# Attention and expert FFN on one Trainium2 core: score products of neighbouring batches interleaved per head pair

## The chip, the core and the metric

The kernel runs on one core of one Trainium2 chip. The metric is the device time of one execution in microseconds (us), as the median of several runs. The engines are named as in the profile: PE is TensorE (its weight loads are PEld), DVE is VectorE, ACT is ScalarE, POOL is GpSimd, SP is the engine that here only issues DMAs (SPq is its queue, ACTq that of ACT).

## What is computed

Eight batches of 128 x 256 go through a cross attention with 8 heads, whose score scale depends on the batch's token count, and then through a two-expert FFN of which the router picks one expert for each row. In short form (the real code reshapes):

```python
x = x + xcond(layernorm(x), ctx, ctx, itok)      # softmax(s * q.T @ k) per head, s = SCALE * log(itok[b])
logits = layernorm(x) @ w_router.T               # 2 experts
h = einsum('nd,ehd->enh', layernorm(x), w_fc)    # 256 -> 2 x 1024
a = square(where(h >= 0, h, 0.5 * h))
expert_out = einsum('enh,edh->end', a, w_proj)   # 1024 -> 256 for each expert
x = x + (expert_out of the chosen expert) * (its softmax weight)
```

## The kernel before

All products are in float32r, and where precision asks for it an operand is split in two: a rounded part (`_hi`, made by ACT) and a remainder (`_lo`, made by POOL or DVE). An FFN product is thus three matmuls (hi x hi, lo x hi, hi x lo).

**Work of one batch b**, in the names of the code. `load_x(b)` and `load_kv(b)` bring the rows in; `x_moments`, ACT's `x_ln` and `x_rstd`, `x_newton` and `q_normalise(b)` make the normalised, scaled q on DVE; `q_part_hi`, `q_part_lo`, `k_part_hi` and `split_k` split q and k. Six DMAs, `stack_q(b, 0..2)` and `stack_k(b, 0..2)`, put the parts above one another in `q_st` and `k_st` (two buffers each, by b % 2), so that one product over 64 rows gives hi x hi and the cross terms. A stack of batch b waits until `scores_kq(b-2, 3)` has been done. Then, for each of four head pairs g:

- `scores_qk(b, g)` (L1158, four matmuls) writes the scores with queries on the partitions into `snp`, and DVE's `row_max(b, g)` (L723) takes the negated row maximum. In batches 0 and 1 odd pairs use `hp` instead, so two are in flight; from batch 2 on there is one place, and `scores_qk(b, g)` waits for `row_max(b, g-1)`.
- When all four maxima are there, DVE splits them (`split_max_hi`, `split_max_lo`), `max_transpose(b)` (L1168) turns them, ACT's `max_rows(b)` copies them to `mx`.
- `scores_kq(b, g)` (L1182 and L1186, eight matmuls) writes the scores with keys on the partitions into `stp`, the maximum already subtracted, and ACT's `exp(b, g)` (L436) makes `probs`. There is one `stp`: `scores_kq` of the next pair waits for the exp of this one.
- `values(b, e)` (L1202, 16 matmuls) multiplies two pairs' probabilities by v. When both halves are done DVE runs the chain `pv_turn`, `den_inverse`, `attention_out`, `attention_turn`, `x2_sum`, `x2_moments`, (ACT: `y_ln`, `y_rstd`), `x2_newton`, `x2_normalise` (L779), which ends in `x2n`.

**Work of one group g of two batches.** `x_transpose(g)` (L1246) needs x2n of both batches, `xt_part_hi` and `xt_part_lo` split it, then 16 chunks `ffn1(g, c)` (L1218, six matmuls) and 16 chunks `ffn2(g, c)` (L1236, six matmuls). Between them ACT has `leaky` and `square_hi`, POOL `square`, DVE `square_lo`; `expert_out` adds the result with the router's coefficient to `y`. The weights come in eight pieces each (`load_weights`), are rounded by ACT (`split_w`) and their remainder is made by POOL for the first matrix (`split_w`) and DVE for the second (`split_w_lo`).

**What sets the order.** Each engine executes its calls in the order in which they stand in a list written out in the code, one list for SP, POOL, ACT, DVE and PE each; nothing is reordered. An engine whose next call waits for a semaphore lets everything behind it wait too. The wait in `scores_qk` that matters most below is this one (`sets` is 2 in batches 0 and 1, else 1):

```python
wait(pe, s_max, PAIRS * b + (g - sets + 1))
```

and in `scores_kq`, `values` and the stacks:

```python
wait(pe, s_exp, PAIRS * b + g)
pe.wait_ge(s_exp, PAIRS * b + PAIRS // 2 * (e + 1))
wait(q, s_st, PAIRS * (b - 1))
```

## Time and profile before

| | us |
|---|---|
| median of 3 runs | 193.11 (193.11 to 193.41) |
| the profiled execution | 194.08 |
| its span, first to last instruction | 192.3 |
| PE busy | 159.3 |
| DVE busy | 141.2 |
| ACT busy | 97.6 |
| POOL busy | 57.2 |

The profile is of one execution. Its span leaves 1.8 us of that execution's time outside. A line number such as L723 is one of the kernel before. A mean granted TensorE clock of 0.973 stands for the whole span.

### The profile page before, as it was taken

The numbers are of one execution on the slowest core, as the hardware profiler recorded it, in microseconds if no ns is written. First come the engines' busy times: TensorE is split into PE (matmuls) and PEld (weight loads), VectorE is DVE, ScalarE is ACT, GpSimd is POOL, SyncE is SP. The second block draws the span as 40 slices with busy tenths as digits, with TensorE's granted clock in tenths as the row PEclk, the third lists the DMA queues.
The fourth block names the chain that finished last, engine by engine and source line by source line (L and its number), as shares of the span: only waits on it lengthen the run. The fifth ranks groups of instructions, "written<-read, shape, count | busy, mean of one in ns | idle before, by whom it ended". The sixth has DMA issues, their size and how long they took to land.

```text
span 192.3 us, 3953 instructions
## 1 busy us (share of the span) xinstructions
PE 159.3 (83%) x1440; PEld 135.2 (70%) x1440; DVE 141.2 (73%) x313; ACT 97.6 (51%) x179; POOL 57.2 (30%) x66
## 2 busy tenths in 40 slices
PE   0044797533899997999999989999999999999991
PEld 0033554312787685787899869997986999999991
DVE  5688954998789999999999999984278774141421
ACT  3402657943478574297437336562647344344520
POOL 6302354731040622210532402420223223244420
PEclk9999999995599999999999999999999999999999
DMA  4466999973000240421300420000010000010001
GB/s 123 168 221 193 261 309 338 263 248 108 0 31 27 78 143 27 159 65 53 114 2 29 143 78 5 27 2 3 0 55 3 0 0 3 0 55 3 0 0 55
DMA packets 18498, 16.31 MB, mean 85 GB/s; under 512 B 1840, under 2 KB 18352, under 8 KB 18480
## 3 DMA queue, kind: packets, MB, share of 16 engines
q1 hardware_dynamic: 17616, 15.28, 25.5%
q10 hardware_dynamic: 864, 0.79, 1.3%
q8 instruction: 11, 0.18, 0.4%
q14 instruction: 7, 0.06, 0.1%
HBM read 8.72 MB, written 1.05 MB: 51 GB/s over the span
## 4 chain that ended last, share of the span: by engine, by line
PE 51%; DVE 26%; issue 7%; SPq 5%; ACT 5%; DMA 4%; DVEq 0%; ACTq 0%
PE ops L1236 19%; PE hp L1218 18%; DVE negm L723 7%; PE pv L1202 5%; PE stp L1182 4%; DVE a_lo L821 3%; PE snp L1158 3%; DVE wproj_lo L843 2%; DMA cst<-consts 2%; DMA wfc_raw<-w_fc_t 2%; PE stp L1186 2%; ACT probs L436 2%; SPq L137 1%; SPq L168 1%; DVE pvt L742 1%
## 5 line engine op out<-in xcount | busy, mean ns | idle before, releaser
L322 POOL TENSOR_TENSOR a_buf<-l_buf 128x512 f32<-128x512 f32 x32 | 34.7, 1085 | 88.4 <-ACT l_buf L444 65.0
L821 DVE TENSOR_TENSOR a_lo<-a_buf,a_hi 128x512 fp32r<-128x512 f32 x32 | 23.1, 726 | 22.5 <-POOL a_buf L322 22.2
L436 ACT ACTIVATE probs<-stp 128x1024 f32<-128x1024 f32 x32 | 32.8, 1024 | 13.2 <-PE stp L1186 12.3
L1218 PE MATMUL hp<-xt_hi,wfc_hi 128*128 128x256 f32 x128 | 38.6, 301 | 0.4 <-issue 0.4
L1218 PE MATMUL hp<-xt_lo,wfc_hi 128*128 128x256 f32 x128 | 36.5, 285 | 0.0
L1218 PE MATMUL hp<-xt_hi,wfc_lo 128*128 128x256 f32 x128 | 36.4, 285 | 0.0
L723 DVE TENSOR_REDUCE negm<-snp 128x4 f32<-128x1024 f32 x28 | 34.1, 1219 | 3.1 <-PE snp L1158 3.0
L444 ACT ACTIVATE l_buf<-hp 128x512 f32<-128x512 f32 x32 | 19.1, 597 | 33.4 <-PE hp L1218 33.0
L1158 PE MATMUL snp<-k_st,q_st 64*128 64x256 f32 x112 | 14.9, 349 | 20.3 <-DMA q_st<-q_lo 10.8
L1236 PE MATMUL ops<-wproj_hi,a_hi 128*128 128x256 f32 x128 | 27.3, 294 | 0.0
L1218 PEld LDWEIGHTS hp<-xt_hi,wfc_hi 128*128 128x128 f32 x128 | 24.8, 193 | 3.0 <-issue 1.7
L1158 PEld LDWEIGHTS snp<-k_st,q_st 64*128 64x128 f32 x112 | 9.9, 216 | 24.0 <-DMA q_st<-q_lo 10.8
L1236 PE MATMUL ops<-wproj_hi,a_lo 128*128 128x256 f32 x128 | 25.7, 282 | 0.0
L1236 PE MATMUL ops<-wproj_lo,a_hi 128*128 128x256 f32 x128 | 25.7, 281 | 0.0
L1218 PEld LDWEIGHTS hp<-xt_hi,wfc_lo 128*128 128x128 f32 x128 | 24.8, 194 | 0.0
L1182 PE MATMUL stp<-q_st,k_st 64*128 64x256 f32 x128 | 21.4, 348 | 4.0 <-ACT probs L436 3.9
L1218 PEld LDWEIGHTS hp<-xt_lo,wfc_hi 128*128 128x128 f32 x128 | 24.6, 193 | 0.0
L451 ACT ACTIVATE a_hi<-l_buf 128x512 fp32r<-128x512 f32 x32 | 20.1, 630 | 4.2 <-PE ops L1236 3.5
L1236 PEld LDWEIGHTS ops<-wproj_hi,a_hi 128*128 128x128 f32 x128 | 19.6, 189 | 2.4 <-issue 0.8
L1182 PEld LDWEIGHTS stp<-q_st,k_st 64*128 64x128 f32 x128 | 13.4, 204 | 9.8 <-ACT probs L436 5.2
L1236 PEld LDWEIGHTS ops<-wproj_hi,a_lo 128*128 128x128 f32 x128 | 19.7, 188 | 0.0
L1236 PEld LDWEIGHTS ops<-wproj_lo,a_hi 128*128 128x128 f32 x128 | 19.7, 188 | 0.0
(73 smaller groups left out, 220.9 us busy)
## 6 DMA issues: line engine op xcount, KB each, us to landing
k_st<-k_hi SPq DMA_DIRECT2D x16, 128.0 KB, 2.1
wfc_raw<-w_fc_t SPq DMA_DIRECT2D x8, 256.0 KB, 5.4
wproj_raw<-w_proj_t SPq DMA_DIRECT2D x8, 256.0 KB, 5.2
q_st<-q_hi SPq DMA_DIRECT2D x14, 128.0 KB, 2.3
x_raw<-x SPq DMA_DIRECT2D x8, 128.0 KB, 2.9
k_st<-k_lo SPq DMA_DIRECT2D x8, 128.0 KB, 2.1
q_st<-q_lo SPq DMA_DIRECT2D x8, 128.0 KB, 2.1
v_raw<-ctx_t SPq DMA_DIRECT2D x8, 128.0 KB, 2.5
```

What stands on the lines that cost most here:

```text
L322: pool.tensor_tensor(a_buf[d % 2][:, :, :], l_buf[d % 2][:, :, :], l_buf[d % 2][:, :, :], ALU.mult).then_inc(s_a, 1)
L436: act.activation(probs[g][:, :, :, :], stp[:, :, :].rearrange("p e (c n) -> p e c n", c=KC), ACT.Exp).then_inc(s_exp, 1)
L444: act.activation(l_buf[d % 2][:, :, :], hp[:, d % 2, :].rearrange("p (c n) -> p c n", c=2), ACT.Prelu, alpha=0.5).then_inc(s_l, 1)
L451: act.activation(a_hi[d % NA][:, :, :], l_buf[d % 2][:, :, :], ACT.Square).then_inc(s_ahi, 1)
L723: dve.tensor_reduce(negm[b % 2][:, :, :, g].rearrange("p c e -> p e c"), pair[:, :, :].rearrange("p e (c n) -> p e c n", c=KC), AX.X, ALU. ...
L821: dve.tensor_tensor(a_lo[d % NA][:, :, :], a_buf[d % 2][:, :, :], a_hi[d % NA][:, :, :].bitcast(f32), ALU.subtract).then_inc(s_alo, 1)
L843: dve.tensor_tensor(w_piece(w_lo, w, n), w_piece(w_raw, w, n), w_piece(w_hi, w, n).bitcast(f32), ALU.subtract).then_inc(s_wlo[w], 1)
L1158: last = pe.matmul(pair[:, e, qc * KEYS:(qc + 1) * KEYS], q_st[j][rows, g, qc * P:(qc + 1) * P], k_st[j][rows, g, :], start=(qc == 0), sto ...
L1182: pe.matmul(stp[:, e, kc * DIM:(kc + 1) * DIM], k_st[j][rows, g, kc * P:(kc + 1) * P], q_st[j][rows, g, :], start=(kc == 0), stop=False, s ...
L1202: last = pe.matmul(pv[32 * g:32 * g + 32, e * DIM:(e + 1) * DIM], v_one[j][:, kc * HEADS + h, :], probs[h // 2][:, h % 2, kc, :], start=(e ...
L1218: last = pe.matmul(hp[:, d % 2, half], wfc[w][:, kc, c * P:(c + 1) * P], xt[:, kc, :], start=(c % 2 == 0 and kc == 0 and w == 0 and xt is ...
L1236: last = pe.matmul(ops_[:, t * DIM:(t + 1) * DIM], a[d % NA][:, c % 2, t * P:(t + 1) * P], wproj[w][:, c, :], start=(c % CH == 0 and part ...
```

## The change

Nothing is added to or taken from what is computed, and the number of matmuls, vector operations and transfers stays. One wait is new, in `q_normalise`, which now may not overwrite `q_f` of two batches ago before `q_part_lo` has read it:

```diff
             def q_normalise(b):
                 j = b % 2
                 dve.wait_ge(s_xsc, b + 1)
+                wait(dve, s_qlo, b - 1)
                 dve.tensor_scalar(q_f[j][:, :], x_raw[j][:, :], xmv[j][:, 0:1], xsc[j][:, 0:1],
                                   ALU.subtract, ALU.mult).then_inc(s_qf, 1)
```

(From there on a line of the changed kernel has a number one higher.) Everything else is the order of the five lists. On PE `scores_qk(2, g)` stands between `scores_kq(1, g)` instead of behind all of batch 1, `scores_qk(3, g)` between `scores_kq(2, g)`, and so on with each next batch:

```diff
             scores_kq(1, 1)
+            scores_qk(2, 0)
             scores_kq(1, 2)
             values(1, 0)
+            scores_qk(2, 1)
             scores_kq(1, 3)
+            scores_qk(2, 2)
             values(1, 1)
-            scores_qk(2, 0)
-            scores_qk(2, 1)
+            scores_qk(2, 3)
+            max_transpose(2)
+            scores_kq(2, 0)
+            scores_kq(2, 1)
+            scores_qk(3, 0)
             x_transpose(0)
```

`x_transpose(0)` has 30 blocks of PE ahead of it where it had 24; `x_transpose(1)` has 79 in both kernels (one ffn2 more, one scores_qk less among them), `max_transpose(6)` 122 where it had 114, `scores_qk(7, 3)` and `values(7, 1)` about the same. Further places that matter: `values(0, 1)` now stands ahead of `scores_kq(1, 0)`, `scores_qk(1, 0)` behind `scores_kq(0, 0)`.

On ACT the head of the list is:

```diff
             load_len()
+            load_router()
             load_kv(act, 0)
             load_kv(act, 1)
-            load_router()
...
             k_part_hi(0)
-            pick_rows()
-            k_part_hi(1)
             q_part_hi(0)
             stack_q(act, 0, 0)
-            stack_q(act, 0, 1)
+            k_part_hi(1)
             x_ln(1)
             x_rstd(1)
+            stack_q(act, 0, 1)
             q_part_hi(1)
+            pick_rows()
```

and between `exp(1, 1)` and `exp(1, 2)` there are now `k_part_hi(4)` and `q_part_hi(4)`; between `exp(2, 0)` and `exp(2, 1)` there are `y_ln(1)` and `y_rstd(1)`, which before stood far ahead of batch 2's exps. POOL's list splits the weights in the same order with the small steps set otherwise.

**PE, from scores_kq(1, 3) on, before** (stp and mx: scores_kq; snp from k_st and q_st: scores_qk; pv from probs: values; pv from x2n: x_transpose):

```order
L1182 MATMUL stp<-q_st1,k_st1 128x256 x2
L1186 MATMUL stp<-mx1,pick 128x256 x2
L1182 MATMUL stp<-q_st1,k_st1 128x256 x2
L1186 MATMUL stp<-mx1,pick 128x256 x2
L1202 MATMUL pv<-probs2,v_one1 32x256 x2
L1202 MATMUL pv<-probs3,v_one1 32x256 x2
L1202 MATMUL pv<-probs2,v_one1 32x256 x2
L1202 MATMUL pv<-probs3,v_one1 32x256 x2
L1158 MATMUL snp<-k_st0,q_st0 128x256 x8
L1246 MATMUL pv<-cst,x2n0 128x128 x2
L1246 MATMUL pv<-cst,x2n1 128x128 x2
L1158 MATMUL snp<-k_st0,q_st0 128x256 x4
```

and the same place in the changed kernel:

```order
L1159 MATMUL snp<-k_st0,q_st0 128x256 x4
L1183 MATMUL stp<-q_st1,k_st1 128x256 x2
L1187 MATMUL stp<-mx1,pick 128x256 x2
L1183 MATMUL stp<-q_st1,k_st1 128x256 x2
L1187 MATMUL stp<-mx1,pick 128x256 x2
L1159 MATMUL snp<-k_st0,q_st0 128x256 x4
L1203 MATMUL pv<-probs2,v_one1 32x256 x2
L1203 MATMUL pv<-probs3,v_one1 32x256 x2
L1203 MATMUL pv<-probs2,v_one1 32x256 x2
L1203 MATMUL pv<-probs3,v_one1 32x256 x2
L1159 MATMUL snp<-k_st0,q_st0 128x256 x4
L1169 MATMUL snp<-cst,nm_r0 128x128 x2
```

Batch 2's scores (snp) moved in front of, between and behind batch 1's products, and the turn of its maxima follows at once; the transpose of x2n comes after two scores_kq of batch 2.

**DVE, from attention_out(1) to x2_normalise(1), before** (yst, ymv, yvar: x2_moments; yn, ysc: x2_newton; negm: row_max; x2n: x2_normalise; the x names are steps of a later batch's q):

```order
L751 TENSOR_TENSOR att_t<-pvt,den_r 128x2x128
L757 STREAM_TRANSPOSE att<-att_t 128x256
L763 TENSOR_TENSOR x2_1<-x_keep1,att 128x256
L661 BN_STATS yst1<-x2_1 128x6
L664 BN_AGGR ymv1<-yst1 128x2
L667 TENSOR_SCALAR yvar1<-ymv1 128x1
L661 BN_STATS xst0<-x_raw0 128x6
L673 SCALAR_TENSOR_TENSOR yn11<-yrs1,yvar1 128x1
L676 TENSOR_SCALAR yn21<-yn11 128x1
L679 SCALAR_TENSOR_TENSOR ysc1<-yn21,yrs1 128x1
L723 TENSOR_REDUCE negm0<-snp 128x2x2
L779 TENSOR_SCALAR x2n1<-x2_1,ymv1,ysc1 128x256
```

and the first part of the same chain in the changed kernel, from row_max(2, 2) on:

```order
L724 TENSOR_REDUCE negm0<-snp 128x2x2
L743 STREAM_TRANSPOSE pvt<-pv 128x512
L724 TENSOR_REDUCE negm0<-snp 128x2x2
L747 RECIPROCAL den_r<-pvt 128x16
L732 CAST nm_r0<-negm0 128x4x4
L737 TENSOR_TENSOR nm_r0<-negm0,nm_r0 128x4x4
L752 TENSOR_TENSOR att_t<-pvt,den_r 128x2x128
L673 SCALAR_TENSOR_TENSOR yn10<-yrs0,yvar0 128x1
L758 STREAM_TRANSPOSE att<-att_t 128x256
L664 BN_AGGR xmv0<-xst0 128x2
L764 TENSOR_TENSOR x2_1<-x_keep1,att 128x256
L676 TENSOR_SCALAR yn20<-yn10 128x1
```

Batch 1's chain now runs among batch 2's last maxima, the split of these, and the newton steps of batch 0 and of a later x; behind the rows shown come x2_moments(1), x_newton(5), x2_normalise(0), x2_newton(1) and x2_normalise(1).

**SP, the head of the list, before** (cst: consts; k_st and q_st: stacks; the last row is the weights):

```order
L137 DMA x_raw1<-x 128x1x256
L188 DMA cst<-consts 128x132
L160 DMA k_st0<-k_hi0 32x4x256
L160 DMA k_st0<-k_lo0 32x4x256
L160 DMA k_st0<-k_hi0 32x4x256
L168 DMA q_st0<-q_lo0 32x4x256
L160 DMA k_st1<-k_hi1 32x4x256
L160 DMA k_st1<-k_lo1 32x4x256
L160 DMA k_st1<-k_hi1 32x4x256
L176 DMA v_raw0<-ctx_t 128x2x128
```

and in the changed kernel:

```order
L137 DMA x_raw1<-x 128x1x256
L176 DMA v_raw0<-ctx_t 128x2x128
L176 DMA v_raw1<-ctx_t 128x2x128
L188 DMA cst<-consts 128x132
L160 DMA k_st0<-k_hi0 32x4x256
L137 DMA x_raw0<-x 128x1x256
L160 DMA k_st0<-k_lo0 32x4x256
L168 DMA q_st0<-q_lo0 32x4x256
L160 DMA k_st0<-k_hi0 32x4x256
L152 DMA wfc_raw<-w_fc_t 128x2x256 x2
L143 DMA kv_raw0<-ctx_kv 128x1x256
L160 DMA k_st1<-k_hi1 32x4x256
```

Both v loads moved to the front, the last stack_k(0, .) moved behind stack_q(0, 2), and two weight pieces and a context load moved in ahead of batch 1's stacks.

## Rows read from the trace of the kernel before

**Rows 1.** The page, section 1: busy time of each engine.

```profile
PE 159.3 (83%) x1440; PEld 135.2 (70%) x1440; DVE 141.2 (73%) x313; ACT 97.6 (51%) x179; POOL 57.2 (30%) x66
```

**Rows 2.** Stretches: us; busy of PE, PEld, DVE, ACT, POOL; clock; DMA share; GB/s.

```profile
10.84:48.00 37.16, 22.22 (x176) 14.13 (x176) 29.48 (x59) 19.33 (x38) 14.32 (x15) 0.93 0.80 241
...
40.10:46.30 6.20, 0.08 (x4) 0.04 (x2) 5.72 (x16) 2.31 (x7) 1.16 (x2) 0.75 0.53 164
...
48.00:53.10 5.10, 4.44 (x21) 3.64 (x20) 3.45 (x9) 2.54 (x7) 0.00 (x0) 0.50 0.01 2
...
53.10:188.30 135.20, 132.60 (x1246) 117.44 (x1244) 100.81 (x225) 71.64 (x125) 38.43 (x39) 1.00 0.12 39
```

**Rows 3.** Waits (us, times, longest): whole span, then two of PEld from 50 us.

```profile
PEld snp L1158 <- DVE negm L723: 10.4, 6, 6.3
...
PEld snp L1158 <- DVE negm L723: 1.8, 2, 1.2
PEld snp L1168 <- DVE nm_r L736: 1.6, 3, 1.1
```

**Rows 4.** Timeline from 38 to 50 us: start, duration, engine, line, operation.

```profile
38.37 1.29 POOL L315 TENSOR_TENSOR wfc_lo<-wfc_raw,wfc_hi 128x512 fp32r<-128x512 f32 x1
...
38.51 1.30 DVE L779 TENSOR_SCALAR x2n<-x,ymv,ysc 128x256 f32<-128x256 f32 x1
...
38.64 1.07 PE L1202 MATMUL pv<-probs,v_one 128*32 128x256 f32 x16 [1.12 <-ACT probs L436]
...
40.20 0.71 DVE L742 STREAM_TRANSPOSE pvt<-pv 128x512 f32<-128x512 f32 x1
...
46.13 0.40 DVE L779 TENSOR_SCALAR x2n<-x,ymv,ysc 128x256 f32<-128x256 f32 x1
...
46.99 1.11 PE L1246 MATMUL pv<-cst,x2n 128*128 128x128 f32 x4
...
49.56 0.55 PE L1218 MATMUL hp<-xt_hi,wfc_hi 128*128 128x256 f32 x1 [0.38 <-issue]
```

**Rows 5.** Timeline from 7 to 11 us: the last stacks of batch 0, PE's start.

```profile
7.61 1.28 ACTq L168 DMA_DIRECT2D q_st<-q_hi  x2
...
8.38 0.53 SPq L168 DMA_DIRECT2D q_st<-q_lo  x1
...
10.84 0.80 PE L1158 MATMUL snp<-k_st,q_st 64*128 64x256 f32 x4 [10.84 <-DMA q_st<-q_lo]
```

**Rows 6.** Groups of instructions: count, busy us, mean ns, idle before and its releaser.

```profile
L723 DVE TENSOR_REDUCE negm<-snp 128x4 f32<-128x1024 f32 x28 | 34.1, 1219 | 3.1 <-PE snp L1158 3.0
...
L399 ACT ACTIVATE k_hi<-kv_raw 128x256 fp32r<-128x256 f32 x8 | 3.3, 408 | 5.9 <-DMA kv_raw<-ctx_kv 5.8
```

**Rows 7.** Timeline from 19 to 32 us: exp(0,0), values(0,1), exp(1,0).

```profile
19.82 1.02 ACT L436 ACTIVATE probs<-stp 128x1024 f32<-128x1024 f32 x1 [1.61 <-PE stp L1186]
...
31.10 1.93 PE L1202 MATMUL pv<-probs,v_one 128*32 128x256 f32 x16
...
31.20 1.02 ACT L436 ACTIVATE probs<-stp 128x1024 f32<-128x1024 f32 x1 [0.56 <-PE stp L1186]
```

**Rows 8.** Timeline at 56 to 58 us: a score pair between two ffn1 chunks.

```profile
56.26 0.28 PE L1218 MATMUL hp<-xt_lo,wfc_hi 128*128 128x256 f32 x1
...
57.05 0.41 PE L1158 MATMUL snp<-k_st,q_st 64*128 64x256 f32 x4
...
57.38 0.38 PE L1218 MATMUL hp<-xt_hi,wfc_hi 128*128 128x256 f32 x1
```

**Rows 9.** Timeline later: x_transpose(1), max_transpose(6), the last expert_out.

```profile
87.72 0.60 PE L1246 MATMUL pv<-cst,x2n 128*128 128x128 f32 x4
...
112.95 0.44 PE L1168 MATMUL snp<-cst,nm_r 128*128 128x128 f32 x2 [0.86 <-DVE nm_r L736]
...
188.26 0.87 DVE L837 SCALAR_TENSOR_TENSOR y<-ops,coef,y 128x256 f32<-128x256 f32 x2 [1.87 <-PE ops L1236]
```

**Rows 10.** The page, section 6: DMA issues, KB each, median us to landing.

```profile
k_st<-k_hi SPq DMA_DIRECT2D x16, 128.0 KB, 2.1
```

## What is predicted

> **What bounds the kernel now.** I read the page's busy times first, then a table by stretch, then who waited for whom, then the timeline of the first 60 us. TensorE (PE) is busy 159.3 us of 192.3, VectorE (DVE) 141.2; no other engine comes near [rows 1]. The stretches say where PE's missing 33 us lie [rows 2]. Up to 10.84 us PE has nothing [rows 5]. From 10.84 to 48.00 it is busy 22.22 of 37.16 us, and inside that lies a hole, 40.10 to 46.30, with 0.08 us of PE work while DVE is busy 5.72 of 6.20 us. From 48.00 to 53.10 the granted clock is 0.50, which is 1.2 GHz. From 53.10 to 188.30 PE is busy 132.60 of 135.20 us at 1.00, 2.4 GHz. So behind 53 us almost every microsecond is PE work that has to be done somewhere, and only three things can shorten the kernel: an earlier start of the dense part, more of its work already done when it starts, and the few waits left in it.
>
> The hole is a wait for DVE. Scores for the next row maximum have one pair of banks, and its weight loads waited 10.4 us in six places for `row_max`, one of 6.3 us [rows 3]. In the timeline values(1,1) starts at 38.64; DVE then takes the turn of that batch at 40.20, the residual, the norm, and only then `row_max(2,0)`; x2n(1) comes at 46.13, x_transpose(0) at 46.99, ffn1(0,0) at 49.56 [rows 4]. After 50 us weight loads still wait 1.8 us for maxima and 1.6 us for their split; those two are DVE being late [rows 3].
>
> **The first part: the start.** Before, the last stack of batch 0 is issued at 8.38 and PE starts at 10.84, 2.5 us later; the two q_hi stacks leave together at 7.61 [rows 5]. Now `stack_q(0,1)` stands on ACT behind k_part_hi(1), 0.41 us [rows 6], and two steps of one column, x_ln(1) and x_rstd(1), with their issue about 0.9 us, `stack_k(0,2)` stands behind `stack_q(0,2)`, one more issue of 0.5 to 0.6 us, and the first context load stands behind the router's. Whichever lands last, PE starts 0.6 to 1.5 us later; I take 0.9, near the single issue and the ACT work, the nearest rows. The two weight pieces, 512 KB, now go out ahead of batch 1's stacks. I cost them at nothing: those stacks are issued from about 11.7 to 16.5 and wanted only near 20, behind four row maxima of 1.22 us each [rows 6]. If that cover is gone, each us of late landing is a us on the path.
>
> **The second part: the exps of batches 0 and 1.** scores_kq(0,0) no longer stands behind scores_qk(1,0), which gives back 0.6 of the 0.9: exp(0,0) at 20.1 against 19.82 [rows 7]. Then values(0,1) is put ahead of scores_kq(1,0). It needs exp(0,3) and takes 1.93 us at this clock; before, scores_kq(1,0) went first and exp(1,0) ran at 31.20 beside it [rows 7]. I get exp(1,0) at 32.0, 0.8 late. From there each exp is followed by one product of 0.6 us and takes 1.02 us, so exps are 2 us apart as before. One new wait: ACT's q_part_hi(4) needs q_normalise(4), which on DVE is behind pv_turn(0), the residual of batch 0 and two x steps, about 35.5 us; it holds exp(1,2) by some 0.4 us. values(1,1) ends near 40.2, against 39.7 before [rows 4].
>
> **The third part: what fills the hole, and what it costs DVE.** Three scores_qk(2,g) now stand between the products of batch 1, so row_max(2,0) and (2,1) run at 35.5 to 38.7, where DVE had other work or idled. Behind values(1,1) DVE has row_max(2,2), pv_turn(1) from 40.8, row_max(2,3) with its wait for PE, the two splits, and then batch 1's chain with batch 0's newtons and x5's between. The old chain from 40.20 to the end of x2n(1) at 46.53 is 6.3 us [rows 4]; take out row_max(2,0) and the x step (1.6), put in row_max(2,3), splits, x2_newton(0), x2_normalise(0), x_newton(5) and the wait for y_rstd(1), which ACT now has behind exp(2,0): about 3.5 to 4. So 8.2 to 8.7 us, x2n(1) near 49.2, x_transpose(0) at 49.4 against 46.99. Queued behind it on PE are scores_kq(2,2) and scores_qk(3,1), at half clock 1.7 us with the transpose 1.1: **ffn1(0,0) at 52.3 against 49.56, 2.7 us later**.
>
> But ahead of it PE has now done 33 blocks instead of 26: three scores_kq, three scores_qk, one max_transpose more. Such a pair costs the dense part 1.0 us: the last product of a chunk starts at 56.26, of which about 0.11 us is its own slot (256 columns at 2.4 GHz), and the next chunk starts at 57.38 [rows 8]. With the transpose, 3.3 us of work is off the dense part. **Break-even is ffn1(0,0) at 52.9; I expect a lead of 0.6 us there.**
>
> **The fourth part: the dense part.** At x2_normalise(1) DVE's list has three more row maxima (3.5 us), two splits, and steps of x4, x5 and x6: 6.9 us more of its work, at a time 2.7 us later. So DVE is 4 us ahead. That takes away most waits for maxima and splits. Walking both lists to x_transpose(1), which stands behind 79 blocks in both (one qk less, one ffn2 more now), I find few waits up to about 74 us and two new ones, both from DVE's order: scores_qk(5,1) waits near 81.5 for row_max(5,0), which stands behind x2_normalise(2), and x_transpose(1) waits near 84 for x2_normalise(3), behind expert_out(0,0) and row_max(5,0); each about 0.9 us. The transpose starts near 85.7 against 87.72 [rows 9], with 0.35 us more done: 2.3 ahead, 1.7 of it gained here. Later max_transpose(6), which waited 0.86 us, stands eight blocks further back and no longer waits [rows 9]; with ffn products clustered differently I keep 0.4 of it. ACT's and POOL's new orders are costed at nothing: squares and exps hide behind PE's chunks of six such slots, 0.7 us, as long as the lead lasts, and if not they stop ffn2 or a scores_kq. The added wait in `q_normalise` on q_part_lo(b-1) costs nothing where q_lo is done by then, true in list order for every b. The tail after the last product, 188.26 to the end, is the same 4 us [rows 9].
>
> **The sum.** 0.6 + 1.7 + 0.4 = 2.7 us off. The profiled execution took 194.08 us, its span 192.3 and 1.8 around it; it would become 191.4. The median of the runs, 193.11, is 1.0 below that execution, so the forecast is 193.11 - 2.7 = **190.4 us**.
>
> **A rule against the change.** The row: at 38.51 an x2_normalise takes 1.30 us beside POOL's 1.29 us split of weights from 38.37, and both end within 0.2 us; at 46.13 the same form takes 0.40 us with POOL quiet [rows 4]. The Trainium skill, page "SBUF — State Buffer", section "SBUF: two separate sides", says that VectorE and GpSimd hold one port pair exclusively for a whole instruction and that the loser blocks fully. The trace agrees in this pair: the loss is the other's full length, 0.9 us. By the mean durations the sum above stands; by the lock, the new place of the chain beside POOL's splits gives the third rival.
>
> **The rivals.**
> First, **the clock helps as well**. The same sixteen products take 1.93 us at 31.10 and 1.07 at 38.64 [rows 4, 7]: PE rose to 2.4 GHz between them though the granted clock reads 1.00 before too. A denser run of products from 21 us on could raise it some 5 us sooner (about 1.3 us on the path), and scores in the hole could spare the 0.50 of 48.00 to 53.10 (half of 5.1 us, 2.5). All of it gives 186.6, half of it 188.5. Against: PE still has only about 3 us of work between 40 and 49.
> Second, **the moved work is just moved**: x2n(1) comes 0.6 us later than I say and DVE's lead meets new waits worth what it removes: 193.1.
> Third, **slower, by the shared port**: POOL's later weight splits, 1.3 us each, follow ACT's roundings between the exps, and DVE's chain to x2n(1) is now longer. Each meeting costs 0.9 us [rows 4]. I allowed one half of one. Two more put ffn1(0,0) at 54.1, over the break-even of 52.9; three, with the two DVE waits near 81 and 84 grown alike, eat the recovery too: 2.7 - 2.7 - 1.5 gives 194.6. It decides from ffn1(0,0) at about 54.6. For it: one such meeting stood on the old chain, and the new one is 2 us longer. Against: row maxima, the largest part of the added work, read PSUM and mean 1.22 us over all 28 [rows 6].
> Fourth, **it does not interleave**: scores_qk(2,0) needs six stacks that may only start once scores_kq(0,3) is done (about 28), six issues of 0.6 us and 2.1 to land [rows 10], so 34 at the earliest; it stands ahead of scores_kq(1,2). If loads in front hold SP to 31, exps of batch 1 slip 2 to 3 us and the kernel ends near 194.5.
>
> **How the numbers follow.** Forecast case, 189.2 to 191.8: 0.48. Clock: 0.17. Only moved, 192.3 to 193.6: 0.12. Shared port: 0.16. Held stacks: 0.07. Two late starts of 1 to 2 us (first part) widen the upper side. The range 187.0 to 194.6 leaves out a tenth on either side. A measurement here tells 0.2% (0.4 us) from no change. Faster by more: the forecast case, the clock, and the lower edge of the moved case, 0.67. Within: most of the rest of the moved case, 0.08. Slower: its upper edge, the port and the held stacks, 0.25.
>
> **What would show it.** Right: PE's start near 11.7; exp(1,0) near 32; no wait of 6 us for `row_max` any more, the longest under 2.5; x_transpose(0) at 49 to 50 with more blocks in front; waits for maxima and splits behind 50 us below 2 us; x_transpose(1) near 85.7; PE's last product near 185.6. Wrong: ffn1(0,0) after 52.9 without a later recovery, or a start after 12.5, or a stretch behind 60 us in which PE idles for DVE or ACT more than 1 us at a time; or a stretch from 44 to 53 at full clock, which would make the gain larger than said.

## The result, and the profile after

The changed kernel takes **187.44 us**, the median of 4 runs (187.27 to 190.15). The kernel before took 193.26 beside it (193.11 to 194.19, 4 runs). The ratio is 0.9686, 95% interval 0.9645 to 0.9726: 5.8 us less, where 2.7 were forecast. The time lies inside the range, but the gain is twice what was said.

Executions of this kernel take from 185.4 to 190.15 us, so two traces of it are read here. The first is the profiled run of the comparison, which took 190.15 us (span 188.0). The second, called e1_change below, is the same kernel profiled again; it took 185.4 us (span 183.2). The median lies between them.

The page of the changed kernel, section 1 (busy us, share of the span, instructions) and the granted clock in 40 slices, which answers to [rows 1]:

```profile
PE 159.0 (85%) x1440; PEld 136.5 (73%) x1440; DVE 132.0 (70%) x313; ACT 93.4 (50%) x179; POOL 57.7 (31%) x66
...
PEclk9999999755559999999999999999999999999999
```

TensorE does the same work; DVE is busy 9 us less with the same instructions: their own times add up to 3.8 us less, and the rest of the 9 is that more of them overlap in the record. Its stretches, and then those of e1_change (us from the start: length; busy of PE, PEld, DVE, ACT, POOL; clock; DMA share; GB/s), which answer to [rows 2]:

```profile
12.73:48.00 35.27, 24.17 (x186) 15.40 (x188) 26.39 (x61) 17.75 (x37) 12.74 (x13) 0.82 0.60 187
...
51.00:54.15 3.15, 3.15 (x23) 2.37 (x21) 2.54 (x4) 1.93 (x3) 0.00 (x0) 0.50 0.26 65
54.15:85.69 31.54, 31.54 (x310) 26.90 (x309) 28.16 (x68) 20.94 (x41) 8.97 (x11) 0.98 0.31 103
85.69:183.60 97.91, 97.91 (x915) 90.11 (x914) 65.51 (x147) 47.67 (x87) 31.08 (x30) 1.00 0.10 32
```

```profile
12.84:43.00 30.16, 19.02 (x182) 12.60 (x182) 25.17 (x57) 16.96 (x35) 12.76 (x13) 1.00 0.65 209
43.00:50.03 7.03, 5.43 (x37) 4.35 (x36) 5.42 (x19) 4.15 (x8) 0.00 (x0) 0.52 0.59 178
50.03:80.92 30.89, 30.89 (x311) 26.23 (x310) 28.15 (x68) 20.96 (x41) 8.99 (x11) 1.00 0.33 104
```

And the two stretches of the kernel before that stand against the last ones, cut at its own ffn1(0,0) and x_transpose(1):

```profile
49.56:87.72 38.16, 36.61 (x345) 29.97 (x345) 34.56 (x73) 24.54 (x45) 9.65 (x11) 0.95 0.21 67
87.72:188.30 100.58, 99.53 (x918) 90.57 (x916) 68.18 (x158) 48.24 (x84) 28.78 (x28) 1.00 0.08 27
```

A run of the kernel has three parts, bounded by three starts on TensorE: ffn1(0,0), x_transpose(1), and the last product.

| start of | before | forecast | after (188.0) | e1_change (183.2) |
|---|---|---|---|---|
| TensorE | 10.84 | 11.7 | 12.73 | 12.84 |
| x_transpose(0) | 46.99 | 49.4 | 51.53 | 47.41 |
| ffn1(0,0) | 49.56 | 52.3 | 54.15 | 50.03 |
| x_transpose(1) | 87.72 | 85.7 | 85.69 | 80.92 |
| last product | 187.82 | 185.6 (185.1) | 183.53 | 178.80 |
| ffn1(0,0) to x_transpose(1) | 38.16 | 33.4 | 31.54 | 30.89 |
| x_transpose(1) to last product | 100.10 | 99.4 | 97.84 | 97.88 |

The forecast's 185.6 was counted from 188.26, which is the start of DVE's expert_out [rows 9] and not of the last product, 187.82; the same 2.7 us off the last product is the 185.1 in brackets, and the 99.4 goes with it.

So the two traces of the change agree behind ffn1(0,0) within 0.7 us, and differ by 4.1 us ahead of it. There the clock is the difference. The granted clock is 0.50, which is 1.2 GHz, in 35 to 54 us in the one, and only in 43 to 50 in the other: from scores_qk(2,0) to ffn1(0,0) that makes 18.4 us against 15.3. The remaining 1.0 us is there when scores_qk(2,0) starts, at 35.76 and 34.77. It comes mostly from the first products, which run at half pace in both and reach full pace about 2 us later in the first trace: values(0,0), sixteen products, in the first and the second:

```profile
26.00 1.93 PE L1203 MATMUL pv<-probs,v_one 128*32 128x256 f32 x16
...
26.11 1.07 PE L1203 MATMUL pv<-probs,v_one 128*32 128x256 f32 x16
```

The waits of the weight loads behind 54 us, which answer to the last two of [rows 3], in the first trace (us in total, times, longest):

```profile
PEld hp L1219 <- issue: 2.3, 6, 0.4
PEld hp L1219 <- ACT l_buf L444: 0.4, 1, 0.4
PEld snp L1159 <- issue: 0.4, 1, 0.4
PEld stp L1183 <- issue: 0.2, 1, 0.2
```

No wait for DVE is left there, neither the old ones nor the two new ones of the forecast.

### The profile page after: what moved, and what is told of

It is laid out like the page before. It is cut to its first block, busy times and chain, and to the rows that moved or that the text cites. A ratio compares the mean times of both kernels' runs of the same rounds, so it can differ in the third digit from the quotient of the medians.

```text
span 188.0 us, 3959 instructions
## 1 busy us (share of the span) xinstructions
PE 159.0 (85%) x1440; PEld 136.5 (73%) x1440; DVE 132.0 (70%) x313; ACT 93.4 (50%) x179; POOL 57.7 (31%) x66
## 4 chain that ended last, share of the span: by engine, by line
PE 81%; DVE 5%; DMA 5%; ACT 3%; issue 2%; SPq 1%; ACTq 0%; DVEq 0%
PE hp L1219 26%; PE ops L1237 26%; PE pv L1203 10%; PE stp L1183 7%; PE snp L1159 6%; PE stp L1187 4%; DVE negm L724 4%; DMA kv_raw<-ctx_kv 3%; ACT probs L436 2%; PE snp L1169 1%; PE pv L1247 1%; DMA k_st<-k_hi 1%; DMA q_st<-q_lo 1%; SPq L160 1%; PE hp L1159 0%
## 5 line engine op out<-in xcount | busy, mean ns | idle before, releaser
L322 POOL TENSOR_TENSOR a_buf<-l_buf 128x512 f32<-128x512 f32 x32 | 35.9, 1126 | 95.0 <-DVE a_lo L822 53.8
L724 DVE TENSOR_REDUCE negm<-snp 128x4 f32<-128x1024 f32 x28 | 34.2, 1222 | 11.8 <-PE snp L1159 11.7
L1219 PE MATMUL hp<-xt_hi,wfc_hi 128*128 128x256 f32 x128 | 38.2, 298 | 0.0
L1159 PE MATMUL snp<-k_st,q_st 64*128 64x256 f32 x112 | 15.5, 362 | 16.3 <-DMA k_st<-k_hi 12.7
L822 DVE TENSOR_TENSOR a_lo<-a_buf,a_hi 128x512 fp32r<-128x512 f32 x32 | 24.0, 758 | 2.2 <-ACT a_hi L451 2.2
L1159 PEld LDWEIGHTS snp<-k_st,q_st 64*128 64x128 f32 x112 | 10.7, 232 | 20.3 <-DMA q_st<-q_lo 15.1
L1183 PE MATMUL stp<-q_st,k_st 64*128 64x256 f32 x128 | 22.0, 357 | 3.4 <-ACT probs L436 2.5
L451 ACT ACTIVATE a_hi<-l_buf 128x512 fp32r<-128x512 f32 x32 | 19.6, 627 | 6.4 <-PE ops L1237 6.3
L1183 PEld LDWEIGHTS stp<-q_st,k_st 64*128 64x128 f32 x128 | 14.3, 219 | 8.4 <-ACT probs L436 4.4
```

Source lines behind the costliest of these rows:

```text
L322: pool.tensor_tensor(a_buf[d % 2][:, :, :], l_buf[d % 2][:, :, :], l_buf[d % 2][:, :, :], ALU.mult).then_inc(s_a, 1)
L451: act.activation(a_hi[d % NA][:, :, :], l_buf[d % 2][:, :, :], ACT.Square).then_inc(s_ahi, 1)
L724: dve.tensor_reduce(negm[b % 2][:, :, :, g].rearrange("p c e -> p e c"), pair[:, :, :].rearrange("p e (c n) -> p e c n", c=KC), AX.X, ALU. ...
L822: dve.tensor_tensor(a_lo[d % NA][:, :, :], a_buf[d % 2][:, :, :], a_hi[d % NA][:, :, :].bitcast(f32), ALU.subtract).then_inc(s_alo, 1)
L1159: last = pe.matmul(pair[:, e, qc * KEYS:(qc + 1) * KEYS], q_st[j][rows, g, qc * P:(qc + 1) * P], k_st[j][rows, g, :], start=(qc == 0), sto ...
L1183: pe.matmul(stp[:, e, kc * DIM:(kc + 1) * DIM], k_st[j][rows, g, kc * P:(kc + 1) * P], q_st[j][rows, g, :], start=(kc == 0), stop=False, s ...
```

## The experiments

Ratios are against the kernel before, run beside each on the same chip (194.0 to 194.7 us as median), with 95% intervals; the chips differ between experiments. "Middle" is the stretch from ffn1(0,0) to x_transpose(1), "rest" the one from there to the last product.

### Where the gain sits

**e1_change**: the changed kernel, nothing edited.

> The changed kernel as it is, once more, for a second profile and an interval. The profile at hand has the granted clock at 0.50 from 35 to 55 us and a span of 188.0, other executions have 185.1. Theory 'clock' (the early products keep TensorE at 2.4 GHz longer in the usual execution): a profile of a usual execution shows 0.50 only for 5 to 10 us, ffn1(0,0) near 51.5 instead of 54.15, x_transpose(1) near 83 instead of 85.69. Theory 'dense part' (the gain lies in waits that are gone behind 55 us): ffn1(0,0) no earlier than 53, and from x_transpose(1) to the last product 98.3 us as in the profile at hand, against 100.5 before. Time 187.3 to 187.6 by both.

187.29 us, ratio 0.964 [0.9557, 0.9723]; the trace is the one above. Both theories hold in part: 0.50 lasts 7 us and ffn1(0,0) comes at 50.03, even earlier than 'clock' said, and the stretch behind x_transpose(1) is 97.88 us, the same as in the slower trace.

**e2_new_then_old** and **e3_old_then_new** cut both kernels' lists at x_transpose(1): e2 has the new order up to there and the old one behind, e3 the reverse (an entry that the first half has done is left out of the second).

```
# on each of the five engines, A = list of the change, B = list of before
# e2:  A up to x_transpose(1), then what is left of B
# e3:  B up to x_transpose(1), then what is left of A
# e12: A up to ffn1(0, 0), then what is left of B
```

> Changed kernel up to x_transpose(1) on every engine, and behind it what is left in the order of the kernel before. My forecast put 2.3 of 2.7 us before this point and 0.4 behind it. If the order behind it is worth nothing (the lead of VectorE is what removes the waits, whichever list follows): 187.4 to 187.8. If the new order behind x_transpose(1) is itself worth about 2 us (100.5 against 98.3 us in the two profiles): 189 to 190, with waits of TensorE for negm, nm_r or probs back behind 86 us.

> The other half alone: kernel before up to x_transpose(1), behind it what is left in the order of the changed kernel. If the late order is worth nothing: 193.0 to 193.5. If it is worth about 2 us by itself: 191.0 to 191.6.

e2: 191.38 us, 0.9868 [0.9808, 0.9929]; middle 32.5, rest 101.0. e3: 196.36 us, 1.0147 [1.0052, 1.0242], slower than before; middle 39.9, rest 102.0. In e3 the seam itself puts a wait on TensorE (line engine waited for: us, times, longest), and in 92 to 95 us the clock falls behind it:

```profile
PE ops L1237 <- DVE y L831: 2.7, 1, 2.7
```

```profile
92.00:95.00 3.00, 2.21 (x10) 2.24 (x11) 3.00 (x6) 0.00 (x0) 1.04 (x1) 0.60 0.00 0
```

So e2 keeps less than half of the gain and e3 none: a seam of two orders brings waits of its own, as large as the gain that it was to locate.

**e12_new_head** cuts earlier, at ffn1(0,0):

> All engines follow the changed lists up to ffn1(0,0) and the order of before behind it (the work that the changed head has already done left out there). Theory: what the part behind gains up to x_transpose(1) (38.2 to 30.9 us from ffn1(0,0)) comes from the work done early and DVE's lead from it, more than from the new order behind: then x_transpose(1) comes 32 to 34 us behind ffn1(0,0), the time is 188 to 190. Rival: the new order behind 50 us is what removes the waits: 34.5 us or more and 191 to 193, since e2_new_then_old with a later seam (191.4) already lost half of the gain.

192.96 us, 0.9877 [0.9831, 0.9923]; middle 34.8, rest 100.07. The middle is 3.4 us shorter than before even under the old order (38.2 to 34.8). About 1.4 of that is the clock and not the work done early: before, the low clock reaches into this stretch, here it ends with ffn1(0,0), and with the clock at 1.00 the old order takes 36.73 (e8_before_warm, below). The new order behind is worth another 3.9 (to 30.9), of which 1.9 us are a wait for a stack that only this seam makes. Its waits of TensorE's weight loads from 49 to 110 us:

```profile
PEld stp L1183 <- ACT probs L436: 3.1, 7, 1.4
PEld snp L1159 <- DMA q_st<-q_lo: 2.3, 2, 1.7
```

Time and middle fit the rival (34.5 us or more, 191 to 193), though by a wait that belongs to the seam; without its 1.9 us the middle would be 32.9 and fit the theory. That question stays half open. The rest is that of before to 0.03 us: what the rest gained, 2.2 us, belongs to the order behind ffn1(0,0) alone.

### The interleaving, taken out and put in alone

```
# e6_no_interleave, in the change            # e16_interleave_before, in the kernel before
  scores_kq(1, 1)                              scores_kq(1, 1)
- scores_qk(2, 0)                            + scores_qk(2, 0)
  scores_kq(1, 2)                              scores_kq(1, 2)
  values(1, 0)                                 values(1, 0)
- scores_qk(2, 1)                            + scores_qk(2, 1)
  scores_kq(1, 3)                              scores_kq(1, 3)
- scores_qk(2, 2)                            + scores_qk(2, 2)
  values(1, 1)                                 values(1, 1)
+ scores_qk(2, 0) to (2, 2)                  - scores_qk(2, 0) to (2, 2)
```

The row maxima move with them on DVE: in e6 behind pv_turn(1), in e16 ahead of x2_moments(0,0), behind x2_moments(0,2) and ahead of pv_turn(1).

> Changed kernel with the first interleaving undone: scores_qk(2, 0..2) behind values(1,1) on TensorE, row_max(2, 0..2) behind pv_turn(1) on VectorE; all else as in the change. My forecast gave the interleaving 0.6 us at ffn1(0,0), and VectorE's lead of 4 us the rest. If so: x_transpose(0) 2 to 3 us later (3.5 us of maxima are back on VectorE's chain), and the kernel 2 to 3 us slower, 189.5 to 190.5. If the gain comes from the order behind and from the clock: under 1 us slower. If TensorE's hole also brings a longer stretch at 0.50: over 3 us slower.

> The kernel before with the interleaving alone: scores_qk(2,0), (2,1), (2,2) stand ahead of scores_kq(1,2), behind values(1,0) and behind scores_kq(1,3) on TensorE, their row maxima ahead of x2_moments(0,0), behind x2_moments(0,2) and ahead of pv_turn(1) on DVE. Theory: what e6_no_interleave lost (4.9 us) is mostly work put into the idle time ahead of ffn1(0,0); here 24 products of 0.21 us in the slow clock's stretch leave the stretch behind 46 us, while 3.7 us of row maxima stand ahead of x2n(1) on DVE: ffn1(0,0) comes at 50 to 52 us, the time is 1 to 3 us less than before. Rival: the row maxima push x2n(1) and x_transpose(0) back by their whole 3.7 us and the stretch behind gains nothing else: no difference or 1 to 2 us slower, since DVE is busy over 2.5 of 3 us throughout 41 to 50 us.

e6: 192.25 us (10 runs), 0.9929 [0.9878, 0.9981]. Taking the interleaving out loses 4.9 us of the 5.8; ffn1(0,0) comes at 57.31, and middle (30.8) and rest (97.88) stay as in the change. It is the third branch of the expectation that came, with the longer stretch at 0.50:

```profile
33.00:57.30 24.30, 15.17 (x102) 9.50 (x103) 12.95 (x34) 8.96 (x19) 6.04 (x6) 0.51 0.41 120
```

How much of the 4.9 us is this clock and how much the row maxima back on DVE's chain was not separated.

e16: 197.91 us, 1.018 [1.0137, 1.0223], slower. My theory there fell, and the rival named too small a loss. TensorE up to 39 us, and from 40 us on, in e16:

```profile
PE snp L1158 <- DMA q_st<-q_lo: 4.4, 1, 4.4
```

```profile
PE pv L1246 <- DVE x2n L779: 5.5, 1, 5.5
```

scores_qk(2,0) stands ahead of scores_kq(1,2) and waits 4.4 us for a query stack that the old load order brings at 36.7 us; two exps of batch 1 slip, values(1,1) starts at 43.02 instead of 38.64, with it x2n(1) slips, and ffn1(0,0) comes at 52.98. Behind that wait the granted clock is at 0.50 from 36 us on, where it was from 43 us on before. In the change the same wait is 2.2 us, and the scores start at 35.76 (34.77 in e1_change). Start and wait of that product in the change:

```profile
35.76 0.80 PE L1159 MATMUL snp<-k_st,q_st 64*128 64x256 f32 x4 [2.23 <-DMA q_st<-q_lo]
```

So the interleaving pays in the change, where its stacks come earlier, and costs 3.5 us in the kernel before, where they do not. The two differ in DVE's order too, and the interleaving in the kernel before with the new loads was not tried; that the loads decide it is read from the wait.

### The start

```
# e4_old_start: the load order of the kernel before, x(2)'s included, and zero_k(1) ahead of place_v(0) on POOL
# e5_old_start_x2_late: the same, and on DVE and ACT
- x_moments(2, 0) ... x_moments(2, 2), x_ln(2), x_rstd(2) ahead of row_max(0, 0)
+ the same behind split_max_lo(0) and max_rows(0)
```

> Changed kernel with the old start: kv loads ahead of the router's on ACT, stack_q(0,1) right behind stack_q(0,0), batch 0's stacks ahead of both v loads and load_x(2). The profile shows k_hi(0) at 7.32 us (before: 5.10) and TensorE's start at 12.73 (before: 10.84). If this is on the path: start at 10.9 to 11.3 and 185.5 to 186.2 us. If other work absorbs it (row maxima, exps in fixed steps): 187.0 to 187.6.

> As the old start of the changed kernel, and on top x_moments(2, .) on VectorE and x_ln(2), x_rstd(2) on ScalarE moved behind batch 0's maxima. In the old-start run TensorE began at 10.49 but row_max(0,0) only at 14.53, because VectorE waited 2.61 us for x(2) in front of it. If that wait was all that ate the start: row_max(0,0) near 11.5, max_transpose(0) near 16.8 instead of 19.1, and 185.0 to 185.8 us. If what follows sets the pace (stacks of batch 2, exps): max_transpose(0) early, but the first ffn1 where it was, 187 us.

e4: 188.52 us, 0.9745 [0.9673, 0.9817]. e5: 186.92, 0.9666 [0.9542, 0.9791]. TensorE starts 2.2 to 2.5 us earlier, and the time is that of the change or worse. In e4 DVE stands at a load that is now late, ahead of its first row maximum:

```profile
12.45 0.43 DVE L661 BATCH_NORM_STATS2 xst<-x_raw 128x6 f32<-128x256 f32 x1 [2.61 <-DMA x_raw<-x]
```

In e5 that is mended, and the rest is swallowed on the way: scores_qk(2,0) still waits 1.6 us for its stack and starts at 34.90. TensorE's first product is not on the path; the stacks of batch 2 are.

### The clock, taken by itself

```
+ warm(n): n products of 256 columns on constants, into banks that nothing uses yet
# e7_warm: 14 ahead of scores_qk(2, 0), 13 ahead of max_transpose(2), 7 ahead of scores_kq(2, 1)
# e8_before_warm: 46 ahead of scores_qk(2, 1), in the hole of the kernel before
# e9_start_and_warm: e5 and e7 together
```

> Changed kernel with 34 added matmuls of 128x256 into a bank that nothing uses yet, in three gaps of TensorE: 14 ahead of scores_qk(2,0), 13 ahead of max_transpose(2), 7 ahead of scores_kq(2,1). They fit into gaps of 2.0, 1.7 and 1.1 us at 2.4 GHz. Theory 'clock': the granted clock stays at 1.00 behind 30 us, saving half of the 5 to 20 us that the profiles of the change show at 0.50 or near it: 184.5 to 185.8, and less spread between executions. If the clock is not what differs: 187.0 to 187.6, or slower by up to 0.5 where a gap is shorter than what fills it.

> Kernel before with 46 such matmuls, 5.4 us at 2.4 GHz, ahead of scores_qk(2,1), in the hole from 40.1 to 46.3. Theory 'clock': the stretch at 0.50 from 44 to 53.1 is gone, ffn1(0,0) near 49.0, x_transpose(1) 2 to 2.5 us earlier, 190.7 to 191.3 us: of the change's gain of 5.8 us some 2 would then be the clock's. If the clock costs nothing there because waits for VectorE take its place: 193.

> The change with the load order of the kernel before at the start (but x(2) still late, as in e5_old_start_x2_late) and 34 extra 256-column products without use in TensorE's idle gaps before 45 us (as in e7_warm). Theory: the late start and the stretch at 1.2 GHz are two separate losses of the change, neither hidden by the other. Then the time is 183.0 to 184.5, against 184.8 for the change with the extra products alone, the first matmul at 10.4, the granted clock 0.99 or more. Rival: with the clock at 2.4 GHz the wait for the chain exp, values, x2n sets ffn1(0,0), and that chain starts from row_max(0,0), which the early start moves little: then 184.5 to 185.3.

e7: **184.82 us** (183.52 to 185.01), 0.9552 [0.9453, 0.9651]. 34 products that compute nothing make the change 2.5 us faster by the medians, and its runs lie within 1.5 us of one another; all four are below the fastest of the eight runs of the change itself. Three stretches of it against those of e1_change:

```profile
41.00:44.00 3.00, 2.69 (x19) 2.11 (x19) 2.97 (x10) 0.22 (x1) 1.57 (x2) 1.00 0.79 261
44.00:47.00 3.00, 2.68 (x27) 2.20 (x27) 2.50 (x15) 2.14 (x6) 0.00 (x0) 1.00 0.83 242
47.00:50.00 3.00, 2.29 (x21) 1.67 (x20) 2.97 (x5) 2.63 (x4) 0.00 (x0) 1.00 0.39 116
```

```profile
41.00:44.00 3.00, 0.95 (x6) 0.72 (x8) 2.96 (x11) 0.90 (x2) 0.82 (x1) 0.87 0.70 238
44.00:47.00 3.00, 1.88 (x18) 1.58 (x16) 1.98 (x12) 1.32 (x3) 0.00 (x0) 0.50 0.86 260
47.00:50.00 3.00, 3.00 (x22) 2.25 (x18) 2.43 (x4) 1.90 (x3) 0.00 (x0) 0.50 0.36 101
```

Five more traces have the change's order up to ffn1(0,0) (e2, e10, e12, e13, e14). Set beside the others, the time from scores_qk(2,0) to ffn1(0,0) follows the time at 0.50 in front of ffn1(0,0): 14.1 us with none (e7), 15.3 with 6.8 (e1_change), 16.3 to 16.8 with 9.1 to 11.2 (the five), 18.4 with 19.0 (the first trace). In the kernel before it does not: ffn1(0,0) comes at 49.56, 49.54 and 49.45 with 6.4, 11.5 and 11.1 us at 0.50 in front of it (before, e3, e15). For most of that time TensorE waits for DVE there, and the wait takes as long at half clock. The change filled the wait with products, and so made itself sensitive to the clock.

e8: 192.98 us (10 runs), 0.9898 [0.9806, 0.999]; the same treatment gives the kernel before about 2 us by the ratio (0.2 to 3.8 by the interval), less than the 190.7 to 191.3 us expected. Its ffn1(0,0) comes no earlier (49.77), its waits for maxima stay, and what is gained lies behind: the middle, with the clock at 1.00, is 36.73 us instead of 38.16.

```profile
49.77:86.50 36.73, 35.10 (x345) 28.56 (x346) 34.62 (x73) 24.50 (x44) 9.76 (x11) 1.00 0.21 69
```

e9: 185.14 us, 0.9512 [0.9477, 0.9548]: the same as e7 within the intervals. The rival of that expectation held: TensorE starts at 10.43 and exp(0,0) runs at 21.21, where e7 starts at 12.74 and has it at 21.51.

### DVE's lead

The forecast said that DVE is 4 us ahead behind ffn1(0,0) and that this takes the waits away. A delay put on DVE measures the lead: what is swallowed is the lead.

```
+ def busy(n):                      # n memsets of 128x1280, each waiting for the one ahead
+     for i in range(n): ... dve.memset(spare[:, :, :], 0.0).then_inc(s_spare, 1)
# e10_busy_change: busy(3) ahead of row_max(3, 2)     # e14_busy1_change: busy(1)
# e11_busy_before: busy(3) ahead of row_max(3, 0)
# e13_busy_warm: e10 and warm(28) ahead of scores_qk(3, 3)
```

> The change with three memsets of 128x1280 on an unused buffer, waiting for each other (about 1.15 us each, 3.5 us on DVE by the 128x1024 memset's 0.91), just ahead of row_max(3,2) at about 62 us. Theory: behind 50 us DVE works ahead of TensorE in the change (its row maxima wait for score products there), so that the waits of the kernel before are gone; a DVE delay of 3.5 us is then mostly swallowed: x_transpose(1) comes 31 to 32 us behind ffn1(0,0) (30.9 without), and the time grows by 0 to 1 us. Rival: DVE and TensorE go in step and each delay is passed on: 33 to 34.5 us and 2.5 to 3.5 us more.

> The kernel before with the same three memsets ahead of its row_max(3,0), at about 58 us. Theory: DVE is the late one there (TensorE waits for negm 1.8 and nm_r 1.6 us behind 50 us), so the 3.5 us are passed on: x_transpose(1) comes 40.5 to 42 us behind ffn1(0,0) (38.2 without) and the time grows by 2.5 to 3.5 us. Rival: it has as much slack as the change: growth of 0 to 1 us in both, and the waits have another cause than DVE's lateness.

> e10_busy_change (the change with 4.2 us more on DVE ahead of row_max(3,2)) with 28 products without use (256 columns each, about 3.0 us) put ahead of scores_qk(3,3) on TensorE, the place where it waited 3.05 us there. Theory: of the 5.1 us by which e10's stretch from ffn1(0,0) to x_transpose(1) grew (30.9 to 36.0), 3.5 are the wait and 1.6 the stretch at 1.2 GHz that it brought; with TensorE kept busy the wait stays and the clock does not fall, so the stretch is 34.0 to 34.7 us, the granted clock from 59 to 65 us is 1.00, and the time 1 to 2 us under e10's. Rival: the further 1.6 us are work that came late behind the wait (DVE's later steps), and stay: 35.5 us or more.

> e10_busy_change with one memset instead of three: about 1.3 us more on DVE ahead of row_max(3,2). Theory: DVE is only 0.7 us ahead of TensorE there (4.2 us of extra work gave 3.5 us of wait), so TensorE waits about 0.6 us, too short for the clock to fall; the stretch from ffn1(0,0) to x_transpose(1) is 31.3 to 31.8 us and the time 0.4 to 1.0 us over the change's. Rival: more of the delay is swallowed on the way (0 to 0.2 us), or a wait of any length brings the lower clock with it (then 32.3 us or more).

e10: 192.95 us, 0.9937 [0.9884, 0.9989], 5.6 us over the change; middle 36.0 instead of 30.9. e11: 199.54, 1.0243 [1.0204, 1.0282], 4.8 us over before; middle 44.4 instead of 38.2. Both expectations fell, and the theory of the lead with them: the three memsets take 4.2 us with their gaps, and both kernels pass on more than that. The place in e10, and the clock behind it (L1168 there is scores_qk, as the edit moved the lines):

```profile
54.63 1.12 DVE L858 MEMSET spare<- 128x1280 f32 x1 [0.21 <-issue]
56.09 1.12 DVE L858 MEMSET spare<- 128x1280 f32 x1 [0.33 <-DVE spare L858]
57.55 1.12 DVE L858 MEMSET spare<- 128x1280 f32 x1 [0.33 <-DVE spare L858]
```

```profile
59.81 0.80 PE L1168 MATMUL snp<-k_st,q_st 64*128 64x256 f32 x4 [3.05 <-DVE negm L726]
```

```profile
59.00:62.00 3.00, 2.19 (x20) 1.09 (x20) 2.84 (x7) 0.00 (x0) 0.00 (x0) 0.62 0.14 47
62.00:65.00 3.00, 3.00 (x27) 2.60 (x20) 1.59 (x6) 0.92 (x3) 0.58 (x1) 0.81 0.79 210
```

In e13 the wait is filled with products, and the same stretches read:

```profile
59.00:62.00 3.00, 3.00 (x34) 2.15 (x33) 2.16 (x6) 0.00 (x0) 0.00 (x0) 1.00 0.26 87
62.00:65.00 3.00, 3.00 (x32) 2.87 (x31) 2.60 (x10) 1.92 (x6) 1.58 (x2) 1.00 0.82 203
```

The middle as a whole mixes in the clock near 50 us, which differs from run to run (e13's is 35.5, the bound that its rival named). The piece around the delay does not: from scores_qk(3,2) to max_transpose(3) it is 5.19 us in e1_change (52.25 to 57.44), 9.81 in e10, 8.74 in e13, 5.55 in e14, and from max_transpose(3) to x_transpose(1) the four agree within 0.02 us (23.47 to 23.49). It falls into two parts at scores_qk(3,3), the product that waits:

| us | e1_change | e14 | e10 | e13 |
|---|---|---|---|---|
| scores_qk(3,2) to scores_qk(3,3) | 2.22 | 2.60 | 5.36 | 5.78 |
| scores_qk(3,3) to max_transpose(3) | 2.97 | 2.95 | 4.45 | 2.96 |

So of 4.2 us of delay 1.1 is swallowed in e10 and 3.1 is passed on, and the clock adds 1.5 behind it, which e13 does not pay. (e13's first part says nothing of the delay: its 28 products run until 60.30, 1.0 us after row_max(3,2) is done at 59.28.) e13 took 190.93 us, 0.9811 [0.9748, 0.9874], 2.0 under e10. e14: 187.94 us, 0.9647 [0.9592, 0.9702], middle 31.6: of 1.3 us of delay 0.4 is passed on, 0.9 is swallowed, and the clock stays at 1.00 (the rest of its longer middle is the low clock, which ends at 51 us there and at 50 in e1_change). **DVE's lead in the change, at this place, is 0.9 to 1.1 us, not 4.**

Why could it not be 4? Each score product of one head pair waits for the row maximum of the pair before, since they share one pair of banks. However early DVE is, it waits for TensorE at the next one, as it does for 11.7 us in all in the first trace (8.6 in e1_change):

```profile
L724 DVE TENSOR_REDUCE negm<-snp 128x4 f32<-128x1024 f32 x28 | 34.2, 1222 | 11.8 <-PE snp L1159 11.7
```

That is 3.0 us in [rows 6]. A lead along the list of an engine is bounded by the buffers between it and the engine that it leads.

### max_transpose(6) alone

```
# e15_before_mt6, the kernel before, TensorE
- max_transpose(6)
  ffn2(1, 1)
  ffn1(1, 9)
+ max_transpose(6)
```

> The kernel before with max_transpose(6) moved two blocks back on TensorE (behind ffn2(1,1) and ffn1(1,9)), nothing else. Theory: its wait of 0.86 us for nm_r is a wait for a DVE result that comes on its own time, so the move takes it away and nothing is late behind it: from x_transpose(1) to the last product 99.2 us instead of 100.1, the time 0.6 to 0.9 us less (ratio 0.995 to 0.997). Rival: max_rows(6), exp(6,0) and scores_kq(6,1) then come late and the wait returns there: 99.8 to 100.3 us, no difference.

193.25 us (12 runs), 0.9932 [0.9898, 0.9965]; rest 99.07 instead of 100.10. As expected: one entry moved by two blocks gives 1.03 us of trace, the whole wait of [rows 9] and a little more. The product has no wait any more:

```profile
113.59 0.38 PE L1168 MATMUL snp<-cst,nm_r 128*128 128x128 f32 x2
```

## Why the prediction was wrong, step by step

**The start (first part): missed by 1.0 us, and it did not matter.** 12.73 instead of 11.7, past the 12.5 that the text had named as a sign of error. My 0.9 leaned on one more issue and on ACT's work, and gave the context load's new place behind the router's no size of its own; k_hi(0) now waits for that load and runs at 7.32 us, where it ran at 5.10:

```profile
7.32 0.42 ACT L399 ACTIVATE k_hi<-kv_raw 128x256 fp32r<-128x256 f32 x1 [1.95 <-DMA kv_raw<-ctx_kv]
```

e4, e5 and e9 show that the loss is covered.

**The exps (second part): right at its end.** exp(0,0), said at 20.1, runs at 21.4 by the late start and by a split of its maxima that takes 0.53 us at 18.22, beside POOL, where 0.17 is usual; but exp(1,0), said at 32.0, stands at 31.72. That is luck: I let values(0,1) take 1.93 us, as before, and it took 1.07, because TensorE had reached full pace by then.

**The hole (third part): filled as said, but what ends it is another thing.** x_transpose(0) was said at 49.4 and came at 51.53 and 47.41, ffn1(0,0) at 52.3 and came at 54.15 and 50.03: that the forecast lies in the middle of the two traces is luck as well. It let DVE's chain to x2n(1) set the time. In both traces DVE waits in that chain for y_rstd(1) (1.15 and 0.91 us), which stands on ACT behind exp(2,0), and is done 0.2 us ahead of x_transpose(0). TensorE meanwhile goes without a gap from scores_kq(2,1), which waits for the same exp, over scores_qk(3,0) to x_transpose(0):

```profile
49.95 0.58 PE L1183 MATMUL stp<-q_st,k_st 64*128 64x256 f32 x2 [1.11 <-ACT probs L436]
...
50.89 0.41 DVE L780 TENSOR_SCALAR x2n<-x,ymv,ysc 128x256 f32<-128x256 f32 x1
...
50.97 0.63 PE L1159 MATMUL snp<-k_st,q_st 64*128 64x256 f32 x4
51.53 1.11 PE L1247 MATMUL pv<-cst,x2n 128*128 128x128 f32 x4
```

Products and exps lie on this path now, and so the clock does. The text treated the 1.2 GHz of 48.00 to 53.10 as fixed. It moves by run, and with it 3 to 4 us.

**The dense part (fourth part): the step that failed.** It held two terms, 1.7 us up to x_transpose(1) and 0.4 behind. The first had two waits in it that do not come and left out the clock; the second was too small.
- Up to x_transpose(1) the forecast's stretch was 33.4 us; it is 30.9 to 31.5. The forecast took 3.0 us of work out of it (three pairs and a transpose less, 0.35 more for an ffn2) and 1.7 of waits: the 3.4 of [rows 3] less two new ones. Against e8_before_warm, the old order with the clock at 1.00, the 7.3 us that e1_change gains here come apart. The clock is 1.4 (38.16 to 36.73). The work is 2.5: three scores_kq, four scores_qk and a max_transpose less and one ffn2 more, at the 0.58, 0.34, 0.14 and 0.72 us that TensorE goes forward by each in these traces. What is left, 3.3, are waits. So the old waits were sized well and the work 0.5 too high, and two things were wrong. Before, 49.56 to 53.10 ran at 1.2 GHz [rows 2] on work of this stretch, for which the forecast had nothing; in the change the low clock ends at 50 to 56 us, at or shortly behind ffn1(0,0) and mostly on other work. And I added two new waits of 0.9 us each, at scores_qk(5,1) and x_transpose(1): neither came. In e1_change the x2n that x_transpose(1) needs is done at 79.99, 0.9 us ahead of it:

```profile
79.57 0.42 DVE L780 TENSOR_SCALAR x2n<-x,ymv,ysc 128x256 f32<-128x256 f32 x1
```

- The reason given, a DVE lead of 4 us, was false (e10, e14). That the old waits went because the new order puts enough products between a row maximum and the score product that needs it, place by place, is argued and not shown: e12 has other waits back when the new head runs under the old order, but part of them are the seam's.
- Behind x_transpose(1) I kept 0.4 of max_transpose(6)'s 0.86 us. Alone it is worth 1.03 (e15). The rest of the 2.2 us, 1.2, is not taken apart by a run. By the lists 0.4 of it is work, the ffn2 that now stands ahead of x_transpose(1) for a scores_qk behind it, which the forecast had as 0.35. For the other 0.8 the trace of before offers a wait of 0.6 us for probs, 0.1 more for a split maximum and 0.4 of issue (weight loads, us in total, times, longest, from 87.72 us):

```profile
PEld snp L1168 <- DVE nm_r L736: 1.2, 2, 1.1
...
PEld pv L1202 <- ACT probs L436: 0.6, 1, 0.6
PEld snp L1168 <- issue: 0.4, 1, 0.4
```

**The sum.** For the slower of the two traces: ffn1(0,0) 4.6 later instead of 2.7, middle 6.6 shorter instead of 4.8, rest 2.3 shorter instead of 0.7: 4.3 off the last product. x_transpose(1) was met to 0.01 us by two errors that cancel. For the faster trace, 0.5 later, 7.3 and 2.2 shorter: 9.0 off. The measured gain of 5.8 lies between. Behind ffn1(0,0) both traces gain 3.4 to 4.0 us more than was said; ahead of it the one is 1.9 us later than said and the other 2.2 earlier.

**The rivals.** The clock was the one that held in part: the forecast case with half of it gives 188.5, all of it 186.6, and 187.4 was measured. But it does not help as I put it. The change does not spare the low clock. It moves it out of the middle, and ahead of ffn1(0,0), where it cost the kernel before nothing, it now costs up to 4 us by how long it lasts. e7 shows that all of it is worth 2.5 us more. The shared port cost nothing on the chain to x2n(1), where the rival had it: both x2n steps on the chain (48.70 and the 50.89 above) take 0.41 us with POOL quiet, where [rows 4] had 1.30.

```profile
48.70 0.41 DVE L780 TENSOR_SCALAR x2n<-x,ymv,ysc 128x256 f32<-128x256 f32 x1
...
46.00:51.00 5.00, 2.96 (x20) 2.28 (x22) 3.71 (x21) 2.22 (x5) 0.00 (x0) 0.50 0.74 211
```

The rule of the Trainium skill, page "SBUF — State Buffer", section "SBUF: two separate sides", that the two hold the port for a whole instruction, is borne out elsewhere in the change. 18 DVE instructions of the first trace run more than 0.15 us and 30% over the median of their kind, each beside a POOL instruction, 9.6 us in all; before it was 23 and 12.1. The clearest is a step of one column that takes 0.22 us at 50.25 and 1.01 here, and ends within 0.02 us of POOL's:

```profile
80.09 1.04 POOL L322 TENSOR_TENSOR a_buf<-l_buf 128x512 f32<-128x512 f32 x1 [3.54 <-ACT l_buf L444]
80.14 1.01 DVE L673 SCALAR_TENSOR_TENSOR yn<-yrs,yvar 128x1 f32<-128x1 f32 x1
```

Row maxima are not among them (mean 1.22 us in both kernels). None of the 18 made TensorE wait behind ffn1(0,0), where no wait for DVE is left; ahead of it one is the split of batch 0's maxima at 18.22, for which TensorE did wait, 0.4 us longer than without it. The held stacks were real but small: scores_qk(2,0) waits 2.2 us for its stack, against 34 us named as the earliest start; 34.77 and 35.76 were seen. e16 shows what it costs when it is larger.

## What to carry to other kernels

A wait of TensorE can have two prices: its length, and the time at 1.2 GHz behind it. Where the profile shows the granted clock at 0.50 behind a gap, ask what work now stands in that time, and try a few products without use in the gap before reordering anything: they gave 2.5 us here, nearly half of what a whole new order gave. Before a lead of one engine is written into a sum, look for the buffer that bounds it. And count the clock's stretches as something that moves with the work ahead of them: of the two traces of the change one is 4.8 us longer, and the clock is all that was found to differ. A low clock was free here while TensorE waited for DVE, and had its price once the wait was filled with products.

## What the runs showed of the hardware

- **Short and long waits.** Behind a wait of 0.3 us (e14) the granted clock stays at 1.00; behind 3.05 us (e10) it reads 0.62 and 0.81 in 59 to 65 us and costs 1.5 us; behind 4.64 us (e11) 0.92, 0.50, 0.50 and 0.94 in 59 to 71 us, and the middle grows by 6.2 us for 4.2 of delay. The Trainium skill, page "TensorE: Matmul & The Clock Gate", part 1, says that an idle array falls back to half rate, and that how many products run slowly at the start varies from run to run. The traces agree with both: in two traces of the change full pace comes at 28 and at 26 us.
- **The low clock outlasts the gap.** In the slower trace it is at 0.50 from 35 to 54 us while TensorE is busy 5.09 of the first 6.00 us, 3.38 of the next 5.00 and all of the last 3.15 before ffn1(0,0):

```profile
35.00:41.00 6.00, 5.09 (x40) 3.30 (x40) 2.70 (x4) 2.05 (x5) 3.54 (x4) 0.52 0.42 123
41.00:46.00 5.00, 3.38 (x24) 1.59 (x24) 3.83 (x7) 2.34 (x6) 2.50 (x2) 0.50 0.56 184
```

- **A granted clock of 1.00 does not say that products run at 2.4 GHz.** In the kernel before the same sixteen products of `values` take 1.93 us at 31.10 and 1.07 at 38.64 with the clock at 1.00 in both places [rows 4, 7]. The trace holds no record of the clock ahead of 32.92 us, and the view prints 1.00 where there is none. In all 18 traces the spacing of the products drops where the first record begins (in values from 87 to 46 ns, in scores_kq from 116 to 67), so until then the pace has to be read from the products. That place moves by itself: 32.92 in the kernel before and 28.08 in e15_before_mt6, which is the same kernel up to there; 28.36 and 26.17 in the two traces of the change. So the 1.07 us of values(0,1) at 29.93 in the change are no effect of its order.
- **DVE and POOL.** The pair at 80.09 above: a DVE instruction can take as long as the POOL instruction beside it, whatever its own size; a row maximum does not (same mean in both kernels).
- **Left open.** Why the low clock begins at 35 us in one execution and at 43 in another of the same kernel was not tried: both have a gap of 2.0 to 2.2 us ahead of scores_qk(2,0). The fastest kernel of the study is e7_warm, 184.82 us; e9_start_and_warm, 185.14, cannot be told from it.
